# Causal row maxima of at most 256 columns: one VectorE reduction for both heads of a slot

## The reference

```python
att = jnp.einsum('bhqd,bhkd->bhqk', q, k) * scale
causal = jnp.tril(jnp.ones((T, T), bool))
att = jnp.where(causal[None, None], att, -jnp.inf)
y = jnp.einsum('bhqk,bhkd->bhqd', jax.nn.softmax(att, axis=-1), v)
```

## Time and profile before

| | |
|---|---|
| runs | 1537.02, 1539.83 and 1545.12 us, median 1539.83 us |
| the profiled execution | 1542.09 us, span from first to last instruction 1540.3 us |
| granted TensorE clock, mean | 0.978 |
| TensorE matmuls busy | 1408.5 us, 91% of the span |
| VectorE busy | 1195.1 us, 78% |
| ScalarE busy | 1057.6 us, 69% |
| row maxima (L1240) | 1536 instructions, 867.5 us of VectorE's busy time |

### The profile page before, as it was taken

The page is one execution under the profiler, slowest core; times in us unless marked ns, Lnnn a source line. Parts: engine busy times, 40 slices in busy tenths (PEclk is TensorE's granted clock), DMA queues, the critical chain, the costliest instruction groups (busy, mean ns, idle before and its releaser), DMA issues.

```text
span 1540.3 us, 37645 instructions
## 1 busy us (share of the span) xinstructions
PE 1408.5 (91%) x14527; PEld 632.2 (41%) x14527; DVE 1195.1 (78%) x2439; ACT 1057.6 (69%) x2139; POOL 655.2 (43%) x535
## 2 busy tenths in 40 slices
PE   3699999999999999999999999999999988689997
PEld 1222323322333433434334344343343432379896
DVE  6788888888877687787877877878778686557784
ACT  2378887788778677687777776776777767346562
POOL 3544664565523322434336234352453221336563
PEclk9699999999999999999999999999999999799999
DMA  5535434434324333333323242333233311077771
GB/s 178 130 94 161 139 110 113 135 103 121 100 57 112 78 114 94 108 112 98 83 84 108 81 117 75 101 98 82 90 104 92 88 37 45 29 259 246 279 241 54
DMA packets 119062, 175.25 MB, mean 114 GB/s; under 512 B 26113, under 2 KB 85735, under 8 KB 114280
## 3 DMA queue, kind: packets, MB, share of 16 engines
q1 hardware_dynamic: 110960, 157.94, 35.3%
q0 software_dynamic: 5888, 14.24, 2.8%
q10 hardware_dynamic: 2048, 0.83, 0.2%
HBM read 101.81 MB, written 51.15 MB: 99 GB/s over the span
## 4 chain that ended last, share of the span: by engine, by line
PE 63%; DVE 19%; ACT 8%; issue 5%; DMA 3%; POOL 1%; SPq 1%; POOLq 0%; DVEq 0%; ACTq 0%
PE psO L761 15%; PE psM L472 12%; DVE negmax L1240 11%; PE psS L784 11%; PE psK L815 7%; PE psK L472 7%; ACT probs L1049 6%; PE psS L472 4%; PE psK L706 2%; DVE xn L1188 1%; DVE mrows L1353 1%; DVE stats L1162 1%; PE psM L900 1%; DMA stack<-mrows 1%; PE psM L851 1%
## 5 line engine op out<-in xcount | busy, mean ns | idle before, releaser
L1240 DVE TENSOR_REDUCE negmax<-psS 128x1 f32<-128x512 f32 (+3 forms) x1536 | 867.5, 615 | 200.5 <-PE psS L784 112.0
L1049 ACT ACTIVATE probs<-psK 128x512 f32<-128x512 f32 (+3 forms) x1536 | 755.4, 546 | 288.4 <-PE psK L815 166.7
L761 PE MATMUL psO<-probs,V 128*32 128x256 f32 (+1 forms) x5632 | 439.5, 384 | 7.4 <-ACT U L1041 5.8
L784 PE MATMUL psS<-stack 48*128 48x512 f16 (+3 forms) x1536 | 282.2, 364 | 47.6 <-DVE negmax L1240 41.9
L815 PE MATMUL psK<-stack 50*128 50x512 f16 (+3 forms) x1536 | 275.2, 355 | 11.0 <-DMA stack<-mrows 5.2
L784 PEld LDWEIGHTS psS<-stack 48*128 48x128 f16 x1536 | 74.0, 93 | 359.7 <-DVE negmax L1240 300.2
L761 PEld LDWEIGHTS psO<-probs,V 128*32 128x32 f32 x5632 | 112.1, 108 | 187.8 <-issue 116.7
L1473 POOL TENSOR_TENSOR rstd<-lnt,minus_half 128x4 f32<-128x4 f32 x24 | 24.8, 1031 | 248.1 <-DVE lnt L1180 248.1
L815 PEld LDWEIGHTS psK<-stack 50*128 50x128 f16 x1536 | 75.4, 94 | 41.9 <-ACT probs L1049 19.7
L1610 POOL DMA_INDIRECT out_dram<-stack,put_to x32 | 76.7, 2398 | 17.9 <-issue 9.1
L472 PE MATMUL psM<-xT,wx 128*128 128x512 f16 x288 | 75.5, 382 | 1.6 <-DVE mrows L1353 0.6
(11 more groups left out here) (198 smaller groups left out, 2027.4 us busy)
## 6 DMA issues: line engine op xcount, KB each, us to landing
spare<-in_L_ffn_w_dram SPq DMA_DIRECT2D x32, 1024.0 KB, 6.3
parts_scratch<-parts SPq DMA_DIRECT2D x192, 128.0 KB
stack<-parts_scratch SPq DMA_DIRECT2D x96, 256.0 KB, 3.8
stack<-parts_scratch SPq DMA_DIRECT2D x96, 128.0 KB, 3.5
packed<-U SPq DMA_DIRECT2D x192, 64.0 KB
recipB<-recip_scratch SPq DMA_DIRECT2D x46, 256.0 KB
shared<-shared SPq DMA_DIRECT2D x48, 128.0 KB, 2.1
probs<-back_scratch POOLq DMA_DIRECT2D x16, 258.0 KB, 3.1
```

Source lines behind the costliest of these rows:

```text
L761: mm = nc.tensor.matmul(psO[32 * i:32 * i + 32, q0:q1], v_of(par)[:, kt, 2 * g + i % 2 + PAIRS * (i // 2), :], probs[:, (unit + i % 2) % P ...
L784: mm = nc.tensor.matmul(psS[:, banks[hh], 0:n], stack_of(par, 0)[rows, hp, qt * P:(qt + 1) * P], stack_of(par, 1)[rows, hp, 0:n], start=Tr ...
L1049: nc.scalar.activation(probs[:, t % P_RING, i, q0:T], psK[:, S_BANKS[t][i], q0:T], ACT.Exp, scale=SM_SCALE / (1 if b.kind == "A" else WSCA ...
L1240: nc.vector.tensor_reduce(negmax[:, g % 2, at:at + 1], psS[:, S_BANKS[u // 2][j], 0:n], AX_X, ALU.max, negate=True).then_inc(s["max_done"], 1)
```

## The change

For a slot of kind B whose heads have at most 256 columns (m % 4 is 0 or 1) and whose second bank is the first one's right-hand neighbour, the two reductions become one. It waits until both heads' scores are there, reads both banks as a 128 x 2 x n operand, writes the two maxima with a stride of 8 columns, and raises `max_done` by two. That holds for the slots m = 0, 1, 4, 9, 12, 13, 16, 21, 24, 25 and 28: 11 of 32 in each of 8 B attentions, 88 pairs. In those slots the wait on `negmax_rows` (for m = 0, 16 and 24) is passed over too.

```diff
                         n = (u % 8 // 2 + 1) * P if kind == "B" else T
+                        first, second = S_BANKS[u // 2]
+                        if n <= 2 * P and second == first + 1:
+                            if j:
+                                continue
+                            dve.wait_ge(s["scores_q"], b.at("scores_q", k + 2))
+                            nc.vector.tensor_reduce(negmax[:, g % 2, at:at + 2 * TT + 1:2 * TT], psS[:, first:first + 2, 0:n], AX_X,
+                                                    ALU.max, negate=True).then_inc(s["max_done"], 2)
+                            continue
                         if u % (S_UNITS // NG) == 0:
```

## The result

The changed kernel took 1545.73 us (median of 20 runs) against 1541.88 for the kernel before beside it: ratio 1.0022, 95% interval 1.0012 to 1.0032. That is 3.4 us (1.9 to 4.9) more, less than the 0.5% that a measurement here tells from no change. Its profiled span is 1544.0 us, 3.7 more than before.

The account below looks back on a forecast made before the run. TensorE was taken to bound the kernel (busy 91%, 63% of the chain). Late loads behind slots 16 and 24 add 2.1 us, slot 4 saves 0.3: +1.8 on the median 1539.83 gives 1541.6 us, range 1535.5 to 1547.0.

Parts of the forecast that it names:

- The bound, and that freed VectorE time is worth nothing: Whole kernel: TensorE busy 91%, chain 63% on it; VectorE's freed 0.76 us a B attention counts nothing except at slot 4.
- The first rival: All merged pairs: VectorE's freed time counts in full, -6.1 us by overlap or -12 by busy time; chance 0.10.
- The durations: Merged instructions: same time as one head with as many elements, 0.42 us for 2 x 128, 0.68 for 2 x 256.
- the third rival: Merged instructions: two-bank reading costs 0.56 and 0.84 us, releases come later still, 6.8 us slower; chance 0.11.
- Slots 16 and 24, short by 0.13: Next slots' score loads: room 0.06 of the 0.19 us needed, so 0.13 later each, 2.1 us over eight B attentions.
- The second rival: Loads behind slots 16 and 24: nothing is gated, only slot 4 counts, -0.3 us; chance 0.13.
- The wait for the second head's scores adds nothing I can see: Start of merged reductions: no added delay, since both heads' mask matmuls are issued as a pair.
- the 0.04 of room in slot 13: Load after slot 13: 0.35 us of room before a later release, enough by 0.04, so no delay.
- Slot 21 hidden behind ScalarE: Load after slot 21: 0.17 us late, absorbed by the exponents' scores' idle 0.25 waiting for ScalarE.
- Slot 4, a gain of 0.3: Slot 4 where experts are routed: the next VectorE step starts 0.05 us earlier, five times, some 0.3 us gained.
- The dropped wait on `negmax_rows` ... costs and frees nothing: Reductions losing that wait: it is for a VectorE step many slots before, so dropping it changes nothing.
- The sum: Whole kernel: 8 x 2 x 0.13 = 2.1 less 0.3, giving +1.8 us.

Follow-up runs that it names:

- Merged where there is room: The change in slots 0, 1, 4, 9, 12, 25 and 28 alone, against the kernel before: ratio 1.0003 (0.9988 to 1.0017).
- the run raised by one: The changed kernel with `max_done` raised by one for a merged pair instead of two, TensorE's waits counted accordingly; ratio to the kernel before 1.0020 (0.9998 to 1.0042).
- the wide ones merged: The change without its bound of 256 columns, so 384 and 512 too, 21 of 32 slots; ratio to the kernel before 1.0151 (1.0122 to 1.0180).

## Why the prediction was right, point by point

- **The bound, and that freed VectorE time is worth nothing:** right. Merged where there is room, three pairs change a B body by -0.02, and the four pairs that lie in the bodies of C leave those as they were. The first rival is out.
- **The durations** 0.42 and 0.68: measured 0.425 and 0.694. Two banks in one operand cost 0.01; the third rival's price was not there.
- **Slots 16 and 24, short by 0.13:** right at the load (0.48 instead of 0.34). The second rival, that nothing is gated, is out by the run of these two alone. But of the 0.13 TensorE kept only some 0.08 in each (0.16 of that run, halved): between the scores of slots 17 and 18, and of 25 and 26, it makes up 0.05. I had let all of it move by 0.13: this term was too large.
- **"The wait for the second head's scores adds nothing I can see":** the step that failed. Where VectorE was idle before the slot, the merged instruction starts 0.10 late (slots 9, 13, 21, 25 and 28): 0.04 for the second head's signal, 0.07 for the wait that the raise by two splits off. That closed the 0.04 of room in slot 13, whose next load came late. The run of slots 16 and 24 and the run raised by one both grow by 0.16 to 0.17, against 0.23 to 0.25: the 0.07 between them is slot 13's (+0.08 against 0.00 and +0.01 in the table).
- **Slot 21 hidden behind ScalarE:** right, with less to spare than I forecast. The load came 0.75 after the reduction's start instead of 0.56, and the start itself was 0.10 late: 0.29 in all, not 0.17. The exponents' wait of 0.25 was gone, where I expected near 0.1 of it to be left, and at slot 23's scores nothing of the delay remained.
- **Slot 4, a gain of 0.3:** wrong. The next step does start 0.33 instead of 0.39 after it, but the bodies of C that kept the full clock both times take 53.61 and 53.60, 53.33 and 53.33. The gain is 0.
- **"The dropped wait on `negmax_rows` ... costs and frees nothing":** wrong in itself. The kernel before without this wait starts slot 0's reduction 0.07 earlier. In the changed kernel the raise by two stands in its place, so nothing of it showed.
- **The sum:** the eight B bodies, all at the full clock, add up to 381.14 us in the second profile of the kernel before, and to 382.77 and 382.91 in the two of the changed one: 1.6 and 1.8 more, where I had 1.8. The terms were others: 8 x 0.16 = 1.3 from slots 16 and 24 and 8 x 0.08 = 0.6 from slot 13, less the 0.35 that VectorE stood still behind the eighth, not 2.1 less 0.3. So the sign and the main term came from the right mechanism, and that the number fits so closely is luck. The first measurement's interval (1.9 to 4.9 us) begins a little above, the second's (-3.2 to +1.5) ends a little below. That the first one's middle lay at 3.4 did not repeat; the traces show falls of the clock of that size in either kernel.

The Trainium skill (Perfetto Trace Analysis, Optimizing Scalar/DVE Operations) was weighed in the prediction. Its advice that smaller instructions may be better where VectorE is not saturated and makes other engines wait is what these runs show: 1.5% slower with the wide ones merged. Of the overhead that it gives for an operation on PSUM, about 125 ns of the engine's time, merging saved about half here, 0.05 to 0.07 us from a pair's start to its end (0.48 to 0.425, 0.76 to 0.694). The busy times of a pair fell by 0.13 and 0.14 (twice 0.278 less 0.425, twice 0.419 less 0.694), but the two heads' reductions had overlapped.

The Trainium skill (VectorE: DVE Perf Modes, The DRAIN you can't avoid) says that a semaphore behind each operation costs nothing extra. That holds here for raises by one: where the first head raised nothing (both banks given back by the second), a pair took 0.48 us as before. The raise by two cost 0.07 us at the start of an instruction that VectorE was free for, and nothing in slots 16 and 24, where VectorE came straight from the slot before.

What stays open: whether the falls of the clock come a little more often with one kernel than with the other (two profiles of each don't tell), why TensorE makes up 0.05 behind slots 16 and 24, and why VectorE stands still for 0.40 behind the eighth B body in some of the kernels.

## What to carry to other kernels

Merging two small instructions also merges what they hand back: look up which engine waits for the first one's buffer, and compare the later release with the room at that place, slot by slot. Time freed on an engine that then waits is worth nothing, however many instructions it was. Where a price is a tenth of a per cent, compare the length of a repeated stretch in the traces, which at the same granted clock repeats to some hundredths of a microsecond, not the total.

## What the runs showed of the hardware that was not expected

- A reduction that raises its semaphore by two, or that has two waits, gets a wait as an instruction of its own and starts 0.07 us later if VectorE was idle (0.51 against 0.44 us after the scores' start in slot 9, 0.42 against 0.35 in slot 0); in slots 16 and 24, where VectorE was busy until then, the start stays at 0.46.
- A reduction that waits for the second of two mask matmuls issued as a pair, instead of the first, starts 0.04 us later (0.44 against 0.40 in slot 9).
- One reduction over two PSUM banks takes 0.01 us more than one of as many columns in a single bank (0.425 against 0.419, 0.694 against 0.682), and 128 x 2 x 512 takes 1.23 us.
